# Attention scores of two heads in the two 64-row halves of TensorE, in a post-layernorm transformer block

## What is computed

```
b, n, d = x.shape                                    # 4, 512, 128;  H = 16 heads of HD = 8
qkv = (einsum('bnd,ed->bne', x, qkv_w) + qkv_b).reshape(b, n, H, 3 * HD)
q, k, v = split(qkv, 3, axis=-1)                     # each transposed to b, h, n, 8
attn = softmax(einsum('bhqd,bhkd->bhqk', q, k) * HD ** -0.5, axis=-1)
out = einsum('bhqk,bhkd->bhqd', attn, v)  ...  out = out @ fc_w.T + fc_b + x
x = layernorm(x + out)
h = silu(lin(x, w1) * s1) * (lin(x, w2) * s2)        # 128 -> 512
h = gelu(lin(h, h1) * t1);  h = gelu(lin(h, h2) * t2)  # 512 -> 512, twice
x = layernorm(x + lin(h, w3) * s3)                   # 512 -> 128
```

## Time and profile before

| | |
|---|---|
| median of 3 runs | 347.95 us |
| the profiled execution | 347.86 us, span 346.1 us |
| TensorE, VectorE, ScalarE, POOL busy | 320.9, 248.3, 237.5, 150.2 us |
| mean granted clock of TensorE | 0.97 of 2.4 GHz |
| DMA | 13.44 MB, 39 GB/s |

### The profile page before, as it was taken

One profiled execution on the slowest core, in us unless ns is written; L12 is line 12 of the kernel. 1 busy time (PEld: TensorE's weight loads), 2 busy tenths in 40 slices (PEclk: granted clock), 3 DMA queues, 4 the chain that ended last, 5 costly groups with the idle time before them and its releaser, 6 DMA issues.

```text
span 346.1 us, 5553 instructions
## 1 busy us (share of the span) xinstructions
PE 320.9 (93%) x1804; PEld 160.1 (46%) x1804; DVE 248.3 (72%) x516; ACT 237.5 (69%) x433; POOL 150.2 (43%) x227
## 2 busy tenths in 40 slices
PE   8588999999999999999999999989999995899981
PEld 6452323423425444234543334625635361389970
DVE  6579998868788758779998767666477420079973
ACT  4365477987788684976778789487699868528340
POOL 8582081820017960715556304634484924310011
PEclk9899999999999999999999999999999999589995
DMA  6641623211210114211120123400100010000011
GB/s 137 200 86 21 183 82 50 45 24 29 45 31 2 33 26 68 46 31 20 42 35 1 17 33 47 78 1 3 30 1 2 1 32 0 2 0 2 0 32 35
DMA packets 17779, 13.44 MB, mean 39 GB/s; under 512 B 2500, under 2 KB 16597, under 8 KB 17749
## 3 DMA queue, kind: packets, MB, share of 16 engines
q1 hardware_dynamic: 17498, 12.85, 18.0%
q10 hardware_dynamic: 251, 0.20, 0.2%
HBM read 5.51 MB, written 1.05 MB: 19 GB/s over the span
## 4 chain that ended last, share of the span: by engine, by line
PE 69%; ACT 8%; DVE 7%; POOL 6%; issue 4%; DMA 3%; SPq 1%; POOLq 0%; DVEq 0%; ACTq 0%
PE bank L435 20%; PE bank L470 15%; PE bank L455 14%; PE bank L446 12%; DVE negmax L787 4%; PE bank L411 3%; DMA h_nat<-in_L_ffn_h_w_dram 3%; ACT prob L641 2%; ACT h_nat L713 2%; POOL act L996 1%; ACT L641 1%; POOL work L985 1%; PE bank L521 1%; PE bank L428 1%; ACT L713 1%
## 5 line engine op out<-in xcount | busy, mean ns | idle before, releaser
L787 DVE TENSOR_REDUCE negmax<-bank 128x1 f32<-128x512 f32 x256 | 162.5, 683 | 42.9 <-PE bank L446 41.2
L641 ACT ACTIVATE prob<-bank 128x512 f32<-128x512 f32 x256 | 136.8, 601 | 32.4 <-PE bank L455 27.7
L446 PE MATMUL bank<-stack 125*128 125x512 bf16 x256 | 87.7, 382 | 0.8 <-DVE negmax L787 0.5
L455 PE MATMUL bank<-stack 128*128 128x512 bf16 x256 | 85.9, 383 | 1.3 <-DMA stack<-mT 0.7
L470 PE MATMUL bank<-prob,v_sb 128*32 128x512 f32 x512 | 73.0, 613 | 4.6 <-ACT prob L641 4.5
L435 PE MATMUL bank<-act,hT 128*128 128x512 f32 (+1 forms) x320 | 74.8, 377 | 1.1 <-POOL act L996 0.9
L435 PEld LDWEIGHTS bank<-act,hT 128*128 128x128 f32 x320 | 52.4, 194 | 9.7 <-POOL act L996 1.7
L455 PEld LDWEIGHTS bank<-stack 128*128 128x128 bf16 x256 | 22.4, 98 | 54.4 <-issue 35.7
L706 ACT ACTIVATE h_nat<-bank,hs_all 128x512 f32<-128x512 f32 (+1 forms) x40 | 22.9, 603 | 32.3 <-PE bank L435 32.2
L446 PEld LDWEIGHTS bank<-stack 125*128 125x128 bf16 x256 | 23.1, 97 | 45.4 <-issue 29.7
L938 POOL TENSOR_TENSOR rstd<-rstd,mhalf 128x4 f32<-128x4 f32 (+1 forms) x10 | 9.6, 958 | 51.1 <-DVE rstd L768 50.8
(11 more groups left out here) (120 smaller groups left out, 352.3 us busy)
## 6 DMA issues: line engine op xcount, KB each, us to landing
stack<-parts SPq DMA_DIRECT2D x124, 48.0 KB
x_in<-in_L_attn_x_dram SPq DMA_DIRECT2D x4, 256.0 KB, 4.8
h_nat<-in_L_ffn_h_w_dram SPq DMA_DIRECT2D x1, 1024.0 KB, 8.7
work<-in_L_ffn_h_w_dram SPq DMA_DIRECT2D x1, 1024.0 KB, 5.6
res<-in_L_attn_x_dram SPq DMA_DIRECT2D x4, 256.0 KB, 2.6
out_dram<-y SPq DMA_DIRECT2D x3, 256.0 KB, 2.3
work<-in_L_ffn_w_w_dram SPq DMA_DIRECT2D x2, 256.0 KB, 3.0
y<-in_L_ffn_w_w_dram SPq DMA_DIRECT2D x1, 256.0 KB, 5.8
```

The source lines that it names most:

```text
L446: nc.tensor.matmul(space("S", n)[:, :], stack[0][0:MROW, h, qt * P:(qt + 1) * P], stack[1][0:MROW, h, :], start=True, stop=True).then_inc( ...
L455: nc.tensor.matmul(space("T", n)[:, :], stack[1][:, h, kt * P:(kt + 1) * P], stack[0][:, h, :], start=True, stop=True).then_inc(ps_st, 1)
L641: nc.scalar.activation(prob[:, n % NP, :], space("T", n)[:, :], ACT.Exp, scale=SCALE).then_inc(emptied("T", n), 1)
L787: nc.vector.tensor_reduce(negmax[:, g % 2, col:col + 1], space("S", n)[:, :], AX.X, ALU.max, negate=True).then_inc(emptied("S", n), 1)
```

## The change

The stacks have 64-row halves: an even head lies in rows 0 to 63 of column block `s // 2`, its odd neighbour in rows 64 to 127 of the same block, so the stacks have 8 blocks instead of 16. A head's 48 rows are followed by 13 rows of zeros (ones), then by the three rows for the maxima. S uses 61 of 64 rows and T all 64. In `S_TILES` even and odd head alternate for the same query tile. The maxima are arranged by halves, and one `mrow` is two DMAs. The first sixteen S keep their zero products, each four standing behind one S. `NP` grows from 12 to 16. All five orders are rewritten; of each the diff shows at most a line (the token K, for zero products on their own, is defined and stands in no order).

```diff
 SP_ORDER = """
-lw lh xin vb zq*2 zk zq zk zq zk zq zk zq mrow zk zq zk zq lh l3 xin mrow more xres spread mrow spread mrow spread mrow spread mrow xres mrow xin
+lw lh xin vb xin zq*5 zk zq zk zq*2 zk mrow zk*2 lh zk l3 mrow more xres xin spread mrow spread mrow spread mrow spread mrow xres spread mrow spread
...
-    MROW = P - NPART
+    TR = 64
+    MROW = TR - NPART
+    HB = H // 2
...
-    NP = 12
+    NP = 16
...
-        S_TILES += [(g, s0 + c, t, c * NT + t) for c in range(ns) for t in range(NT)]
+        S_TILES += [(g, s0 + 2 * c + e, t, (e * ns // 2 + c) * NT + t) for c in range(ns // 2) for t in range(NT) for e in range(2)]
...
+    def half_of(s, rows):
+
+        return slice(TR * (s % 2), TR * (s % 2) + rows)
...
-        stack = [sb(f"stack{i}", [P, H, N], BF16) for i in range(2)]
+        stack = [sb(f"stack{i}", [P, HB, N], BF16) for i in range(2)]
...
-                            sp.dma_start(stack[i][0:SR, h, :], parts[i][at:at + HD, :, :]).then_inc(rep[j], 16)
+                            sp.dma_start(stack[i][half_of(h, SR), h // 2, :], parts[i][at:at + HD, :, :]).then_inc(rep[j], 16)
...
-                    sp.dma_start(stack[0][MROW:P, s0:s0 + ns, :], mT[0:m_rows(n), 0:P]).then_inc(mrow[n % NG], 16)
+                    rows = m_rows(n) // 2
+                    for e in range(2):
+                        sp.dma_start(stack[0][TR * e + MROW:TR * e + TR, s0 // 2:(s0 + ns) // 2, :],
+                                     mT[rows * e:rows * (e + 1), 0:P]).then_inc(mrow[n % NG], 16)
...
-                    nc.tensor.matmul(space("S", n)[:, :], stack[0][0:MROW, h, qt * P:(qt + 1) * P],
-                                     stack[1][0:MROW, h, :], start=True, stop=True).then_inc(ps_s, 1)
+                    nc.tensor.matmul(space("S", n)[:, :], stack[0][half_of(h, MROW), h // 2, qt * P:(qt + 1) * P],
+                                     stack[1][half_of(h, MROW), h // 2, :], start=True, stop=True).then_inc(ps_s, 1)
                     if n < 16:
                         keep_busy(4)
...
-                    nc.tensor.matmul(space("T", n)[:, :], stack[1][:, h, kt * P:(kt + 1) * P],
-                                     stack[0][:, h, :], start=True, stop=True).then_inc(ps_st, 1)
+                    nc.tensor.matmul(space("T", n)[:, :], stack[1][half_of(h, TR), h // 2, kt * P:(kt + 1) * P],
+                                     stack[0][half_of(h, TR), h // 2, :], start=True, stop=True).then_inc(ps_st, 1)
...
+                    nm, left = (a.rearrange("p (e c) -> p e c", e=2) for a in (nm, left))
+                    hi, mid, lo = (mparts[:, 0:NPART * w].rearrange("p (e m c) -> p e m c", e=2, m=NPART)[:, :, i, :] for i in range(NPART))
```

More of the change, by code:

```diff
@@ L8 @@
 SP_ORDER = """
-lw lh xin vb zq*2 zk zq zk zq zk zq zk zq mrow zk zq zk zq lh l3 xin mrow more xres spread mrow spread mrow spread mrow spread mrow xres mrow xin
-spread*2 mrow spread mrow spread mrow xres spread mrow*2 spread*2 mrow spread out mrow xres mrow*2 out*4
+lw lh xin vb xin zq*5 zk zq zk zq*2 zk mrow zk*2 lh zk l3 mrow more xres xin spread mrow spread mrow spread mrow spread mrow xres spread mrow spread
+mrow spread mrow spread mrow*2 spread xres mrow spread*2 out mrow spread mrow xres mrow*2 out*4
@@ L35 @@
+W*2 Y:3
 """
 ACT_ORDER = """
[L38 to L41, removed]
+x q*2 da wt da x wt*2 zk wm zk wm wt wm wt*2 wm*2 m mrow wm e m e*14 m e q*2 x e*2 wt e wt e wt e wm e*2 wt e*2 wt e m e wm e*2 wm e*2 wm e*2 wm e*2 o
@@ L56 @@
+gl u gh gl u gh gl m h0 u l0 h0 l0 u p2 h0 l0 h0 l0 gh*4 gl*4 p1*2 p2*3
 """
@@ L343, in first_spread @@
                 at = HD * head_of(h)
-                eng.dma_start(stack[i][0:SR, h, :], parts[i][at:at + HD, :, :]).then_inc(rep0[h], 16)
+                eng.dma_start(stack[i][half_of(h, SR), h // 2, :], parts[i][at:at + HD, :, :]).then_inc(rep0[h], 16)
         block = ctx.enter_context(nc.Block())
@@ L412, in transpose4, with keep_busy @@
                 return last
-            def keep_busy(times):
+            def keep_busy(times, into=banks[-1]):
                 for _ in range(times):
-                    nc.tensor.matmul(banks[-1][:, 0:P], wz[:, :], wz[:, :], start=True, stop=True)
+                    last = nc.tensor.matmul(into[:, 0:P], wz[:, :], wz[:, :], start=True, stop=True)
+                return last
             pe.wait_ge(wz_ok, 1)
@@ L601, in step @@
                     nc.tensor.transpose(space("hs", 0)[:, 0:4 * NK + 1], hs_nat, ident[0:4 * NK + 1, 0:4 * NK + 1]).then_inc(ps_hs, 1)
+                elif what == "K":
+                    until_free(pe, "K", n)
+                    keep_busy(4, space("K", n)).then_inc(emptied("K", n), 1)
                 elif what == "L":
@@ L656, in _ @@
                     if n:
[L657 removed]
+                        act.wait_ge(mrow[(n - 1) % NG], 16 * 2 * ((n - 1) // NG + 1))
                     nc.scalar.activation(mT[0:m_rows(n), 0:P], space("m", n)[:, :].bitcast(BF16)[0:m_rows(n), 0:P], ACT.Copy).then_inc(emptied("m", n), 1)
@@ L676, in _ @@
                     until_empty(act, "m", n)
-                    act.dma_start(stack[0][MROW:P, s0:s0 + ns, :], mT[0:m_rows(n), 0:P]).then_inc(mrow[n % NG], 16)
+                    rows = m_rows(n) // 2
+                    for e in range(2):
+                        act.dma_start(stack[0][TR * e + MROW:TR * e + TR, s0 // 2:(s0 + ns) // 2, :],
+                                     mT[rows * e:rows * (e + 1), 0:P]).then_inc(mrow[n % NG], 16)
                 elif what == "a":
@@ L733, in k_ones @@
             def k_ones(j):
-                nc.vector.memset(stack[1][:, GH * j:GH * (j + 1), :].rearrange("p h n -> p (h n)").bitcast(F32), TWO_ONES).then_inc(ones, 1)
+                nc.vector.memset(stack[1][:, 2 * j:2 * j + 2, :].rearrange("p h n -> p (h n)").bitcast(F32), TWO_ONES).then_inc(ones, 1)
             nc.vector.memset(wz[:, :], 0.0).then_inc(wz_ok, 1)
@@ L921, in _ @@
             for j in range(NG):
-                nc.gpsimd.memset(stack[0][:, GH * j:GH * (j + 1), :].rearrange("p h n -> p (h n)").bitcast(F32), 0.0).then_inc(zeros, 1)
+                nc.gpsimd.memset(stack[0][:, 2 * j:2 * j + 2, :].rearrange("p h n -> p (h n)").bitcast(F32), 0.0).then_inc(zeros, 1)
             for what, n, _ in walk(POOL_ORDER):
@@ L959, in _ @@
                     nm, left = negmax[:, n % 2, 0:w], mres[:, 0:w]
-                    hi, mid, lo = (mparts[:, i * w:(i + 1) * w] for i in range(NPART))
+                    nm, left = (a.rearrange("p (e c) -> p e c", e=2) for a in (nm, left))
+                    hi, mid, lo = (mparts[:, 0:NPART * w].rearrange("p (e m c) -> p e m c", e=2, m=NPART)[:, :, i, :] for i in range(NPART))
                     nc.gpsimd.tensor_copy(hi, nm).then_inc(m_step, 1)
```

62 lines of the change are left out of this document (31 added, 31 removed).

## The result

The changed kernel takes 333.27 us in the median of four runs (330.27 to 334.93), against 347.7 before; the ratio is 0.960, with a 95% interval of 0.951 to 0.968. The forecast was 334. The profiled execution took 334.62 us, its span is 332.8, 13.3 us less than before.

A forecast was written before the change was run, and what follows sets the result against it. TensorE was taken to set the pace from 39 to 266 us, VectorE close behind. 347.9 - 15.8 (stretches) - 1 (start) + 2.5 (tail) = 333.6, so 334 us, range 322 to 351.

The forecast's parts named there:

- Part 1: S and T products of different row halves overlap fully, side by side, saving 41.9 us of TensorE in the stretches.
- Rival A: Pairs overlap less, each run of products losing 0.1 us to a weight load: 341 us, chance 0.20.
- Part 2: 147 more array-shape changes in the stretches at 0.1 us: +14.7 us; ends 0.09 (-1.5 us) and 0.14 (+5.9 us).
- Part 3: Eight stretches cut at every 32nd S: 246.8 us become 231.0, saving 15.8, with VectorE next bound in 2, 3, 4, 6.
- Part 4: Zero products behind each of the first sixteen S cost nothing, hidden by VectorE; 3 us if VectorE were not the bound.
- Part 5: SP's copies into the stacks start at about 15.2, not 10.87, yet first S comes earlier: -1 us, between +1 and -1.8.
- Part 6: Two DMAs instead of one per transposed group of row maxima, 17 more: taken as 0, at most 17 x 0.8 us.
- Part 7: From 265.9 us to the end, TensorE needs 60.6 instead of 58.1 us: +2.5 us.
- Rival B: Row halves do not overlap at all, so changes of shape are pure cost: 364 us, slower, chance 0.12.
- Rival C: TensorE waits more, three engines being nearly equal, or its clock falls: 345 us, no difference, chance 0.16.
- The working by stretches: Each stretch takes the larger of TensorE's counted time / 0.96 and VectorE's busy time / 0.92; the first stays as is.

The follow-up runs named there:

- one-half kernel: The changed kernel with all S and T products reading rows 0 to 63 only, so none can lie side by side; 376.35 us, ratio 1.081 to the kernel before.
- full-height kernel: The changed kernel with S and T reading the stack's full height (125 and 128 rows), so they cannot overlap; 344.10 us, ratio 0.987 to the kernel before.

## Why the prediction was right, point by point

- **Part 1, overlap: right.** The pair takes 0.22 us, the partner starts 0.01 us later. Of 198 products counted in the order as starting beside another, the trace shows 184; ten more start 0.05 to 0.17 us behind their neighbour, and some records can be missing. Rival A's price, 0.1 us per run for a weight load, is not there: the loads of the two halves start together too, at 102.79 and at 104.35.
- **Part 2, changes of shape: right in kind, low in size.** A change costs 0.14 us by the one-half and full-height kernels, where 0.1 was taken; the way into an H run costs 0.18, the way back 0.09. That was 6 us too little by part 2's own upper end, and stretches 5, 7 and 8, where TensorE is the bound, came out 0.2, 0.3 and 1.0 us over the forecast. The page "TensorEngine Tiling (Array Packing)" of the Trainium skill says (Tiling Modes) that the engine drains at each change. The trace agrees: by the medians each way between score products and full-height ones is longer than before, by 0.09 to 0.20 us.
- **Part 3, stretches: right in the sum, partly by luck.** 231.4 against 231.0, and stretches 2 to 8 each within 2.8 us. VectorE stands at 88% to 96% in 2, 3, 4 and 6, but TensorE is busy for 91% to 97% there, so that VectorE alone sets the pace is not shown. I held VectorE to 92%; it reached 96% in stretch 3, and without the clock's fall 97% in stretch 4 of the kernel without zero products (29.63 of 30.59 us). Stretch 4 met its 34.2 only with that fall: the six other versions of this kernel without it took 30.6 to 31.6 there.
- **Part 4, zero products at nothing: wrong,** by some 4 us in all and 2 us at the first T. The reason given, VectorE as the bound, holds for the S among themselves. I didn't follow the order on to the transpose of the first maxima, which stands behind 13 of these S and on which the first T hangs.
- **Part 5, start -1 us: wrong,** measured +0.85. In other kernels with the same start the first S came at 19.3 to 19.5, and with the old start at 18.6 to 19.7, so the two starts differ by less than one execution from the next. The copies started 1 us later than worked out, and from the issue to the use of the first one 3.8 us passed, not the 2.1 of a small lone DMA.
- **Part 6, the second DMA: right** for the program's time, not for the first T, which it holds up by 1.2 us.
- **Part 7, tail +2.5:** measured +1.2.
- **Rival B** is what the one-half kernel shows: 376 us against the 364 worked out, by a fall of the clock that was not in it. **Rival C** took a part: two falls of 3.4 us, one of them at 112.5, and a fall between 40 and 250 us was the sign named for C.

So the mechanism was right, pairs against changes of shape, and its size roughly so. That the total met 334 within 1 us is luck: with zero products that really cost nothing, as part 4 assumed, the kernel takes 328.87, 5 us less than forecast. The zero products, a first S later than forecast and a fall of the clock on one side, and a VectorE that let the stretches run closer than 92% on the other, cancelled.

The working by stretches can't be carried to an order that was not made for these prices: it gave 332 to 336 for the old order, which took 350, with changes of shape at 0.1 us where they cost 0.14, and with the waits and the clock left to a fixed 0.96.

## What to carry to other kernels

Products that use at most half the rows can be laid side by side by their rows alone: here a pair saves 0.217 us and a change of array shape costs 0.14. Count both in the order before anything else; with the same halves, 139 pairs against 92 more changes gained, and 125 pairs against 132 more did not. Write the order anew for long runs, and give filler products the shape of their neighbours. Work that another engine's pace hides is hidden only as long as nothing behind it in the order is waited for from elsewhere, here the first maxima.

## What was not expected of the hardware

- A change between the full array and its halves costs more on the way into a run of float32 products (0.18 us) than on the way back (0.09).
- The clock fell after shorter waits than in the kernel before. There it fell after 3.77 us without work; in the changed kernel at 34.0, behind a wait of 1.50 us, and at 112.5, behind one of 2.09 us, for 3.4 us each. A wait of 1.31 us at 109.5, in the kernel with 64-row zero products, had no fall behind it.
- The one-half kernel ran at 1.2 GHz for 34 us while TensorE was never idle; in the full-height kernel, with the same order, the clock fell at 33.8 too but came back after 3.4 us. Fifty products of zeros in 64 rows held the clock in the gap at the start just as full-height ones did; behind the first sixteen S the clock fell earlier with 64-row ones (28.8) than with full-height ones (34.0), in traces where TensorE also waited more. What kept it down in the one-half kernel stays open.
